# Letting the DMA convert an int32 adjacency matrix to bytes, issued from GpSimd

## What is computed

```
h  = inlayer2 @ W.T + b
f1 = h @ w1 + b1 ; f2 = h @ w2 + b2
logits = f1[:, None] + f2[None, :]                       # 4096 x 4096
coefs  = softmax(leaky_relu(logits) + (-1e9) * (1 - (adj > 0)), axis=-1)
x = x + coefs @ layernorm(x)                             # adj: 4096 x 4096 int32
x = x + experts(layernorm(x))                            # 8 experts, top 2 of a softmax gate
```

## Time and profile before

| | |
|---|---|
| median of three runs | 579.19 us |
| the profiled execution | 580.46 us |
| its span (first to last instruction) | 578.7 us |
| PE / DVE / ACT / POOL busy | 79% / 81% / 60% / 13% of the span |
| adjacency DMAs | 256 of 256 KB, median 12.8 us from issue to landing |
| bytes moved by DMA | 94.83 MB, mean 164 GB/s |

### The profile page before, as it was taken

One profiled execution on the slowest core, in us unless ns is written; L12 is line 12 of the kernel. 1 busy time (PEld: TensorE's weight loads), 2 busy tenths in 40 slices (PEclk: granted clock), 3 DMA queues, 4 the chain that ended last, 5 costly groups with the idle time before them and its releaser, 6 DMA issues.

```text
span 578.7 us, 6487 instructions
## 1 busy us (share of the span) xinstructions
PE 458.4 (79%) x1668; PEld 213.6 (37%) x1668; DVE 469.5 (81%) x754; ACT 348.8 (60%) x455; POOL 75.4 (13%) x52
## 2 busy tenths in 40 slices
PE   0520088755993689999979889997999999999996
PEld 0520053322441234444424334352443444444442
DVE  3689987737982989999877878957798989889885
ACT  0644096425552526757474472346989888888884
POOL 3907900300005910000000000001000000000000
PEclk9955579986997579999999999997999999999999
DMA  9999789999999998999999990035243355455321
GB/s 192 219 225 225 162 187 221 221 247 216 222 244 230 226 225 199 220 220 221 221 219 221 221 220 10 1 74 110 73 114 93 91 121 118 91 116 119 91 72 36
DMA packets 39954, 94.83 MB, mean 164 GB/s; under 512 B 5840, under 2 KB 11904, under 8 KB 39936
## 3 DMA queue, kind: packets, MB, share of 16 engines
q1 hardware_dynamic: 38688, 94.52, 74.4%
q10 hardware_dynamic: 1248, 0.10, 0.2%
HBM read 92.38 MB, written 2.23 MB: 163 GB/s over the span
## 4 chain that ended last, share of the span: by engine, by line
PE 35%; DMA 23%; DVE 12%; ACT 10%; issue 8%; SPq 2%; DVEq 0%; ACTq 0%
DMA stage<-in_adj 19%; PE bank L1055 10%; ACT mask L492 5%; PE bank L1100 4%; PE bank L1102 4%; PE bank L1101 4%; PE bank L1089 4%; PE bank L1091 4%; PE bank L1090 4%; DVE c L885 3%; DVE Y L746 3%; SPq L298 2%; DMA x<-in_x 2%; DMA share<-shares 1%; ACT stage L608 1%
## 5 line engine op out<-in xcount | busy, mean ns | idle before, releaser
L1055 PE MATMUL bank<-c,Y 128*128 128x512 f32 x512 | 242.8, 623 | 28.8 <-DVE c L885 28.7
L885 DVE SCALAR_TENSOR_TENSOR c<-g_row,r_col,maskT 128x512 f32<-128x512 uint8 (+1 forms) x256 | 190.9, 781 | 8.8 <-PE bank L1055 6.6
L492 ACT ACTIVATE mask<-stage,sig_bias 128x2048 uint8<-128x2048 int32 x59 | 117.7, 1998 | 94.6 <-DMA stage<-in_adj 66.6
L1055 PEld LDWEIGHTS bank<-c,Y 128*128 128x128 f32 x512 | 95.2, 197 | 158.4 <-DVE c L885 81.1
L608 ACT ACTIVATE stage<-bank,b1T 128x512 f32<-128x512 f32 x128 | 83.8, 688 | 24.2 <-PE bank L1091 22.6
L922 DVE TENSOR_TENSOR stage<-stage,share 128x1024 f32<-128x1024 f32 x64 | 78.3, 1223 | 22.4 <-ACT stage L608 16.0
L928 DVE TENSOR_TENSOR maskT<-stage,maskT 128x1024 f16<-128x1024 f32 x64 | 78.4, 1225 | 0.0
L687 DVE STREAM_TRANSPOSE maskT<-mask 128x512 uint32<-128x512 uint32 x64 | 45.0, 706 | 36.3 <-ACT mask L492 35.9
L615 ACT ACTIVATE maskT<-stage 128x1024 f16<-128x1024 f32 x64 | 67.4, 1053 | 3.3 <-DVE stage L922 3.2
L1100 PE MATMUL bank<-maskT,w2h 128*128 128x512 f16 x128 | 49.1, 384 | 5.8 <-DVE maskT L928 5.3
L1101 PE MATMUL bank<-maskT,w2h 128*128 128x512 f16 x128 | 49.0, 383 | 0.0
(11 more groups left out here) (149 smaller groups left out, 420.2 us busy)
## 6 DMA issues: line engine op xcount, KB each, us to landing
stage<-in_adj SPq DMA_DIRECT2D x256, 256.0 KB, 12.8
share<-shares SPq DMA_DIRECT2D x16, 1024.0 KB, 8.0
share<-in_L_gnn_inlayer SPq DMA_DIRECT2D x8, 256.0 KB, 6.4
share<-in_x SPq DMA_DIRECT2D x4, 512.0 KB, 16.2
out<-c SPq DMA_DIRECT2D x8, 256.0 KB, 4.0
share<-in_L_ffn_W SPq DMA_DIRECT2D x1, 1024.0 KB, 17.8
x<-in_x SPq DMA_DIRECT2D x1, 256.0 KB, 9.1
W_sb<-in_L_gnn_W ACTq DMA_DIRECT2D x1, 64.0 KB, 3.8
```

The lines of the kernel that those rows point to most:

```text
L492: act.activation(mask[:, p % 2], stage[:, p % SLOTS], ACT.Sigmoid, bias=sig_bias[:], scale=1000.0).then_inc(conv_done, 1)
L885: dve.scalar_tensor_tensor(c[:, k % CR].rearrange("p (s i) -> p s i", i=32), g_row[:, bass.ds(s * ST, ST)].rearrange("p (s i) -> p s i", i ...
L1055: mm(bank[:, par, :], Y[:, k], c[:, k % CR], start=(k == 0), stop=(k == NK - 1)).then_inc(c_used, 1)
```

## The change

The conversion goes into the transfer. GpSimd issues the adjacency DMAs with an int32 source and a uint8 destination, four for each supertile (one a quadrant, 2 MB of source each) straight into `mask`, which becomes 8 slots of 128 rows, two whole supertiles. `stage`, `conv_done` and every conversion on ACT, DVE and GpSimd are gone. Because the bytes are now the low values of `adj` and not exactly 0 or 1, the mask is applied with a minimum and not a product. The transposes are twice as large and half as many (four for each supertile, after every eighth chunk), and each waits for all four transfers of its supertile. SP's other loads have no adjacency pieces among them any more. The load of a supertile waits until the supertile that used its slots has been transposed, and stands at a fixed place in GpSimd's program. `h`, `hw` and `cwR` move to the memory of `mask`. TensorE's eight warm-up matmuls no longer wait for the conversions.

```diff
-    PR = 64
+    PR = 128
-    SLOTS = 4
+    SLOTS = 8
+    STEPS = 8
-        stage = sb("stage", [P, SLOTS, PS_, QJ], I32)
-        mask = sb("mask", [P, 2, PS_, QJ], U8)
+        mask = sb("mask", [P, SLOTS, PS_, QJ], U8)
@@ SP
-            def load_adj(s, p):
-                need(sp, conv_done, s * NP + p - SLOTS + 1)
-                for q in range(Q):
-                    sp.dma_start(stage[32 * q:32 * q + 32, p % SLOTS], adj_v[s * NP + p, q]).then_inc(adj_in[p % SLOTS], 16)
...
@@ GpSimd
+            def load_adj(s, par):
+                need(pool, turned, (s - 1) * NP)
+                for q in range(Q):
+                    pool.dma_start(mask[32 * q:32 * q + 32, par * NP:par * NP + NP].rearrange("a p s j -> a (p s) j"),
+                                   adj_v[s, q]).then_inc(adj_in[par], 16)
+            load_adj(0, 0)
             pool.wait_ge(g_copied, 1)
...
             pool.partition_all_reduce(all_max[:], part_max[:], P, RMAX).then_inc(amax_ready, 1)
+            load_adj(1, 1)
...
             pool.tensor_tensor(all_l[:], all_rows[:], all_h[:], ALU.subtract).then_inc(all_ready, 1)
+            load_adj(2, 0)
             split(b2_sb[:], b2h[:], b2l[:])
...
+            load_adj(3, 1)
             split(w1raw, w1h[:], w1l[:], arrived=(w_in, 32))
             split(w2raw, w2h[:], w2l[:])
+            with pool.Fori(2, NS // 2) as i:
+                load_adj(i * 2, 0)
+                load_adj(i * 2 + 1, 1)
@@ DVE
-            def turn(s, p, par):
-                dve.wait_ge(conv_done, s * NP + p + 1)
+            def turn(n, p, par):
+                dve.wait_ge(adj_in[par], 64 * n)
                 dve.transpose(at32v[:, par, PS_ * p:PS_ * p + PS_, :].rearrange("p s w -> p (s w)"),
-                              mask32[:, p % 2]).then_inc(turned, 1)
+                              mask32[:, par * NP + p]).then_inc(turned, 1)
...
-                        at[:, par, :, k // 4, k % 4, :], ALU.max, ALU.mult).then_inc(c_ready, 1)
-                    if k % 4 == 3 and not last:
-                        turn(s + 1, k // 4, 1 - par)
+                        at[:, par, :, k // 4, k % 4, :], ALU.max, ALU.min).then_inc(c_ready, 1)
+                    if k % 8 == 7 and not last:
+                        turn(n, k // 8, 1 - par)
@@ PE
-            pe.wait_ge(conv_done, NP - 1)
```

More of the change, by code:

```diff
@@ L58, in gnn_moe_kernel @@
     LAG = 3
-    assert D == P and NS % 2 == 0 and E % 4 == 0 and FC == 2 and NP == 2 * SLOTS
+    assert D == P and NS % 2 == 0 and E % 4 == 0 and FC == 2 and SLOTS == 2 * NP
     with ExitStack() as ctx:
@@ L115, in gnn_moe_kernel @@
         lgl = sb("lgl", [P, TS, E])
-        sig_bias = sb("sig_bias", [P, 1])
         r_col = sb("r_col", [P, NK])
@@ L149, in gnn_moe_kernel @@
         lower = sb("lower", [4 * E, 1])
-        stage32 = stage[:].rearrange("p a b c -> p (a b c)").bitcast(F32)
-        h = stage32[:, 0:2 * FC * ST].rearrange("p (r f t) -> p r f t", r=2, f=FC)
-        hw = stage32[:, 2 * FC * ST:4 * FC * ST].rearrange("p (r f t) -> p r f t", r=2, f=FC)
+        hid = mask[:].rearrange("p a b c -> p (a b c)").bitcast(F32)
+        h = hid[:, 0:2 * FC * ST].rearrange("p (r f t) -> p r f t", r=2, f=FC)
+        hw = hid[:, 2 * FC * ST:4 * FC * ST].rearrange("p (r f t) -> p r f t", r=2, f=FC)
+        cwR = hid[:, 4 * FC * ST:4 * FC * ST + 3 * P].rearrange("p (b t) -> p b t", b=3)
         at32 = maskT[:].rearrange("p a b c d e -> p (a b c d e)").bitcast(F32)
@@ L166, in gnn_moe_kernel @@
         cwT = gr[0:4 * E, 1920:1920 + N // 2].bitcast(F16)
-        cwR = stage32[:, 4 * FC * ST:4 * FC * ST + 3 * P].rearrange("p (b t) -> p b t", b=3)
         wb = share3[:, :].rearrange("p (e t) -> p e t", e=E)
@@ L187, in gnn_moe_kernel @@
         w_in = sem("w_in")
-        adj_in = [sem(f"adj_in{i}") for i in range(SLOTS)]
+        adj_in = [sem(f"adj_in{i}") for i in range(2)]
         pool_const = sem("pool_const")
@@ L220, in gnn_moe_kernel @@
         dve_step = sem("dve_step")
-        conv_done = sem("conv_done")
         turned = sem("turned")
@@ L272, in by_chunk @@
             return t.rearrange("(q b a e) d -> q a b e d", q=Q, b=NB, a=32, e=4)
-        adj_v = adj.rearrange("(t s i) (q j) -> t q i s j", s=PS_, i=32, q=Q)
+        adj_v = adj.rearrange("(t s i) (q j) -> t q i s j", s=ST // 32, i=32, q=Q)
         out_v = out.rearrange("(n t p) d -> n p t d", t=TS, p=P)
@@ L281, in gnn_moe_kernel @@
         ROWS = (1, 2, 5, 6, 7, 0)
-        CONV_POOL, CONV_DVE = (0,), (1, 2, 3, 6)
         AHEAD = 8
@@ L303, in _ @@
                                  by_chunk(in2)[q].rearrange("a b e d -> a b (e d)")[:, b:b + half]).then_inc(in2_in[b // half], 16)
-            load_adj(0, 0)
             for q in range(Q):
                 sp.dma_start(dst_k(x_j, q), by_chunk(x)[q].rearrange("a b e d -> a b (e d)")).then_inc(xj_in, 16)
-            for p in range(1, NP):
-                load_adj(0, p)
             x_rows = x.rearrange("(n p) d -> p n d", p=P)
[L311 to L315, removed]
             sp.wait_ge(f2_made, 2)
             sp.dma_start(x2[:, 0:TS], x_rows[:, 0:TS]).then_inc(xn_in[0], 16)
-            load_half(1, 1)
-            load_half(2, 0)
             sp.dma_start(x2[:, TS:NK], x_rows[:, TS:NK]).then_inc(xn_in[1], 16)
-            load_half(2, 1)
-            load_half(3, 0)
             sp.wait_ge(y_rows, NK + 1)
@@ L327, in _ @@
             sp.dma_start(w2raw, W2.rearrange("e (c f) d -> f (e c) d", c=FC)).then_inc(w_in, 16)
[L328 to L331, removed]
             def share_out(g):
@@ L410, in _ @@
                                    ALU.mult).then_inc(prod2_ready, 1)
-            for p in CONV_POOL:
-                pool.wait_ge(adj_in[p % SLOTS], 64 * (p // SLOTS + 1))
-                pool.tensor_scalar(mask[:, p % 2], stage[:, p % SLOTS], 0.0, None, ALU.is_gt).then_inc(conv_done, 1)
             pool.wait_ge(pmax_ready, 1)
             pool.partition_all_reduce(all_max[:], part_max[:], P, RMAX).then_inc(amax_ready, 1)
+            load_adj(1, 1)
             pool.wait_ge(mv1_ready, 1)
@@ L485, in _ @@
                 act.dma_start(dst, src).then_inc(small_in if n < 4 else late_in, 16)
[L487 to L493, removed]
             for n in range(2):
@@ L562, in supertile @@
             def supertile(s, par, first=False, last=False):
-                for p in range(NP):
+                for p in range(STEPS):
                     if first:
@@ L568, in supertile @@
                                            scale=ru[:, k:k + 1]).then_inc(y_rows, 1)
-                    if not last:
-                        convert(s + 1, p)
                     if p == 6 and first:
@@ L586, in supertile @@
                         post_d(s - 1)
[L588 to L591, removed]
             act.wait_ge(y_rows, AHEAD + 1)
@@ L659, in _ @@
             dve.memset(ones[:], 1.0)
-            dve.memset(sig_bias[:], -500.0)
             link(dve.memset(eps[:], LN_EPS))
@@ L711, in _ @@
             dve.tensor_reduce(part_max[:, 2:3], nf2[:], AX_X, ALU.max).then_inc(pmax_ready, 1)
-            convert(1)
             dve.wait_ge(amax_ready, 1)
@@ L729, in _ @@
             ins.then_inc(mv1_ready, 1)
[L730 to L734, removed]
+            for p in range(2):
+                turn(1, p, 0)
             dve.wait_ge(ru_exp, 2)
@@ L750, in _ @@
                 row_chunk(k)
[L751 to L754, removed]
+            for p in range(2, NP):
+                turn(1, p, 0)
             POST = 3
@@ L872, in _, with supertile @@
             BN = (12, 13, 17, 18)
-            def supertile(s, par, first=False, last=False):
+            def supertile(s, par, n, first=False, last=False):
                 router = route_b(*ROUTE[0])
@@ L909, in supertile @@
                         next(router, None)
-            supertile(0, 0, first=True)
+            supertile(0, 0, 1, first=True)
             with dve.Fori(0, NS // 2 - 1) as i:
-                supertile(i * 2 + 1, 1)
-                supertile(i * 2 + 2, 0)
-            supertile(NS - 1, 1, last=True)
+                supertile(i * 2 + 1, 1, i + 2)
+                supertile(i * 2 + 2, 0, i + 2)
+            supertile(NS - 1, 1, 0, last=True)
             def weigh(j, e, st):
```

## The result

The changed kernel takes 532.65 us (median of four runs, 527.33 to 533.37) against 578.55 for the kernel before (four runs). The ratio is 0.919, with a 95% interval of 0.9125 to 0.9258. Some executions of a kernel run at a lower granted clock and take longer; all times here are medians of the others. The profiled execution took 533.37 us, its span 531.7.

A forecast was written before the change was run, and what follows sets the result against it. Adjacency transfer bounds attention. Supertile 1 ends at 161.5, supertiles 2 to 6 add 156.5, the last 35.3: attention ends at 353.3 against 387.6, 34.3 us less, so 546.2 profiled, 545 median; range 533 to 599.

The forecast's parts named there:

- What bounds the kernel: Attention stage: bound by the adjacency transfer at 220 GB/s, 38.1 us a supertile, where compute could run at 31.3.
- The rate R: Adjacency loads: the new converting transfer reads 310 GB/s, taken from a stretch at 312, so 27 us for a supertile.
- my own break-even: Steady part: time equals the kernel before at 227 GB/s; compute binds fully from 268, above which the time is the same.
- x lands later: +10: Head: all of load 0 competes with x from another queue, so DVE starts near 37.5 and not 27.7, +10 us.
- the second one (-2.4): Head, between the statistics and GpSimd's chain: two DVE conversions and four transposes become two larger transposes, -2.4 us.
- The stretch that was to stay: Head: from GpSimd's chain at 47.1 to 71.4, holding the eight rows of L746, claimed unchanged.
- my 2.7: Head, behind the rows of Y: conversions and transposes become fewer, larger transposes, -2.7 us.
- The wait for load 2: Supertile 1: load 2, issued behind the split of the sum, lands at 134, wanted near 120; 14 us lost.
- the weight split: GpSimd's 23.7 us holding DVE move behind load 3, mostly inside the wait for load 2, some 2 us outside.
- the rate stays at 220: Rival: the engine's handling of a 4 KB packet, not the write side, takes the time; 595 us, chance 0.16.
- conversion is slow: Rival: converting or building descriptors in software is slow, 141 GB/s, some 135 us more, 714 us; chance 0.13.
- the likeliest case: The forecast itself, 536 to 555 us at chance 0.50; its own range is given as 534 to 556.

The follow-up runs named there:

- Experiments 1 and 2: 1: kernel before, each adjacency DMA writing 128 partitions, 539.28 us; 2: changed kernel, float32 destination and a quarter of the rows, 524.83 us in one run.
- experiment 7: Changed kernel with two idle GpSimd operations added between the products and the all-reduce: 538.39 us in one run.
- experiment 3: Changed kernel with the split of the expert weights moved off GpSimd to ACT (high halves) and DVE (low halves): 526.69 us.
- experiment 4: Changed kernel with load 2 issued before GpSimd waits for PE's sum: 532.39 us; with the edit of experiment 3 as well: 525.70 us.

## Why the prediction was right and wrong

**What bounds the kernel** held. Transfer, not compute, set the pace, and a free supertile costs 31.3 us, met within 0.1 us in all five. Experiments 1 and 2 show that the 220 GB/s was a limit of writing.

**The rate R, 310, was mis-sized: it is 416 to 424.** The row that I took the earlier trace rows was itself a mixture of narrow and wide writes, so it was no upper bound, though I used it as one. By my own break-even it did no harm in the steady part, where anything over 268 is the same. It did harm at load 2.

**The term "x lands later: +10" failed, and it is most of the miss.** x let DVE go at 31.64, 4.0 later than before, not 10. The forecast charged load 0 by the bytes that it reads. Between 4 and 31.7 us GpSimd's queue took 57% of the engines' time and SP's 47%, near equal turns, as I had assumed; but what load 0 moved in it was 1.50 MB written for 6.0 MB read. And of these 4.0 us only 0.8 reached the all-reduce (36.23 against 35.44). Before, the all-reduce stood 3.3 us behind its input, in the lead time of experiment 7, which GpSimd's conversion on L413 had pushed into the path. I had let the removal of that conversion go at nothing. GpSimd's chain then began at 47.00, as before (47.12), where the forecast had 54.7.

The other terms of the head: the second one (-2.4) showed on DVE only. There the stretch from the all-reduce to the last operation ahead of the rows of Y went from 11.8 to 9.9 us, but GpSimd's chain began 1.2 us after its last input (45.8), so it gained 0.9 and not 2.4. The stretch that was to stay (chain to last row of Y) took 22.6 us and not 24.3, and one operation less of DVE lay beside the chain (L742 took 6.98 us there before; on L696 it now takes 0.19 ahead of it). From the rows of Y to the first tile it took 5.1 before and 2.3 now, 2.8 less against my 2.7. First tile: 71.87, forecast 81.4. Supertile 0 took 31.7 against 31.1 (its own terms, 81.4 + 28.8 + 2.5, make 112.7 and not 112.5).

**The wait for load 2 and the weight split were assigned the wrong way round.** The forecast gave 14 us to the wait and 2 to the part of the split outside it. The trace shows 1.16 of waiting and about 15 of hold; experiment 3 shows that it is hold, experiment 4 that removing the wait alone gains nothing. Load 2 was in at 119 and not 134, because it was issued 9.5 us earlier (96.5) and was in 22 us later, where I had 28. The sum came out at 47.7 against 49.0: two errors that cancelled.

**The small rest.** The last supertile took 34.2 and not 35.3. Its 35.3 before were not free of the mask's road, as the forecast had it: DVE's last transpose waited for ACT's conversion, and the first tile came at 352.29, just at the end of the supertile before it. Now the first tile comes 1.2 us ahead of that end, and from first tile to end it takes 35.5 us in place of 35.3. From the end of attention to the end of the span it is 189.6 and not 191.1. I had said that this does not change, and 1.5 us of it did: in the 25 us that begin 12.9 us behind the end of attention PE was granted 0.94 before and 1.00 now. Why the clock differs there was not tried.

Sum of the misses: 8.9 (end of supertile 0), 1.3, 1.1 and 1.5 are 12.8; 546.2 - 12.8 = 533.4, the profiled time.

**The rivals.** That the rate stays at 220 and that conversion is slow are both refuted by the 416 to 424 GB/s read; experiments 1 and 2 add why. The range missed at its lower end: I had let the likeliest case reach down to 534 for "x not delayed and the wait for load 2 shorter", but both together with a faster rate is what happened, and these go the same way.

## What to carry to other kernels

A steady transfer rate well below what another shape of write reaches in the same trace (220 against 312 GB/s here) points at the destination; price a DMA that writes all partitions, before removing bytes. Where writing binds, charge a transfer by the bytes that it writes. When a mixed stretch serves as the upper bound for a rate, it is an average, and the true bound lies above it. Where two engines contend, the same operation can cost many times its free time (23.37 us against 2.13 here), and the cost hides under whatever wait lies over it: take both away before judging either, and look at what else shares the queue of whatever is moved forward.

## What the runs showed of the hardware

- A converting DMA (int32 to uint8, 4 KB read and 1 KB written for a row, 32 partitions) reads 416 to 424 GB/s; int32 to float32 through the same queue, 4 KB written for a row, moves 226. GpSimd's issue took 0.67 us for a DMA of 512 rows.
- An int32 load that writes 128 partitions moved 327 GB/s where one that writes 32 moved 220.
- The all-reduce on GpSimd ran 5.79, 6.16 and 7.85 us after the engine's last operation with its input ready, and 0.14 us after its input when the engine had been free for 11.8 us. GpSimd's next computation started 10.3 to 14.5 us after the all-reduce in the changed kernel and its variants, with a DMA issue of 2.8 us in between. With float32 transfers its inputs had been ready for 3.1 us by then, in experiment 7 for 5.1. What it does there was not tried.
- Eight DVE operations of 0.27 us each took 23.37 us beside a GpSimd chain and 2.13 us ahead of it.
